# A fused attention and feed-forward kernel: the inverse roots of three norms in one chain of tensor-by-tensor steps, with new orders of work on all engines

## The reference

```python
x = x + _layernorm(_L0_attn_ref(_layernorm(x), Wq, Wk, Wv, Wp, bp, rel_table))
x = x + _layernorm(_L0_ffn_ref(_layernorm(x), W_r, W_k, W_v, mu_r, mu_k))
# attention, 16 heads of 64:
scores = einsum('bhtd,bhsd->bhts', q, k) * scale + bias[None]     # bias by clipped distance, causal
out = softmax(scores) @ v, then out @ Wp + bp
# feed-forward: x_prev is x one token earlier
r = sigmoid((mu_r * x + (1 - mu_r) * x_prev) @ W_r.T)
k = (mu_k * x + (1 - mu_k) * x_prev) @ W_k.T
out = r * (square(relu(k)) @ W_v.T)
# every norm:
(x - m) / sqrt(v + 1e-05)
```

## Time and profile before

| | us |
|---|---|
| median of 3 runs | 2222.81 |
| lowest and highest of them | 2222.11, 2223.51 |
| span of the profiled execution | 2224.4 |
| PE busy in it | 2111.2 (95%) |
| DVE busy | 1945.6 (87%) |
| POOL busy | 1697.1 (76%) |
| ACT busy | 1685.6 (76%) |

### The profile page before, as it was taken

The page is one execution under the profiler, slowest core; times in us unless marked ns, Lnnn a source line. Parts: engine busy times, 40 slices in busy tenths (PEclk is TensorE's granted clock), DMA queues, the critical chain, the costliest instruction groups (busy, mean ns, idle before and its releaser), DMA issues. The chain is left out here.

```text
span 2224.4 us, 75124 instructions
## 1 busy us (share of the span) xinstructions
PE 2111.2 (95%) x29456; PEld 1432.2 (64%) x29456; DVE 1945.6 (87%) x5210; ACT 1685.6 (76%) x2529; POOL 1697.1 (76%) x1372
## 2 busy tenths in 40 slices
PE   3798889999999999999999999999999999999986
PEld 1355556666676666667766666776666676666665
DVE  6777778999999999999999999999999998888857
ACT  2478788777878877887787788778877878877734
POOL 4376777788888888888888888888888887777752
PEclk9899999999999999999999999999999999999988
DMA  7111112232322323232232333223232322212251
GB/s 176 30 50 45 41 44 67 53 76 70 74 61 63 71 57 74 71 74 61 64 71 55 75 71 74 61 65 70 56 74 70 75 59 57 59 50 67 66 110 42
DMA packets 336784, 147.13 MB, mean 66 GB/s; under 512 B 172976, under 2 KB 335664, under 8 KB 336432
## 3 DMA queue, kind: packets, MB, share of 16 engines
q1 hardware_dynamic: 336432, 142.33, 26.9%
HBM read 24.25 MB, written 43.06 MB: 30 GB/s over the span
## 5 line engine op out<-in xcount | busy, mean ns | idle before, releaser
L1736 POOL TENSOR_TENSOR probs<-probs_f,probs 128x1024 f16<-128x1024 f32 (+3 forms) x704 | 1121.0, 1602 | 340.4 <-ACT probs L1002 338.0
L984 ACT ACTIVATE probs_f<-score_ps,score_unit 128x1024 f32<-128x1024 f32 (+3 forms) x704 | 620.6, 882 | 240.0 <-DVE score_ps L1293 114.9
L1277 DVE TENSOR_REDUCE row_max<-max_ps 128x2 f32<-128x1024 f32 (+2 forms) x640 | 632.4, 1005 | 17.2 <-PE max_ps L692 14.3
L1002 ACT CAST probs<-probs_f 128x1024 f16<-128x1024 f32 (+3 forms) x704 | 566.9, 814 | 12.3
L726 PEld LDWEIGHTS misc<-v_pair,probs 128*128 128x128 f16 x4608 | 415.0, 97 | 40.0 <-issue 29.1
L726 PE MATMUL misc<-v_pair,probs 128*128 128x65 f16 x4608 | 438.5, 194 | 0.6 <-issue 0.6
L727 PE MATMUL misc<-v_pair,probs 128*128 128x64 f16 x4608 | 436.8, 193 | 0.0
L728 PE MATMUL misc<-v_pair,probs 128*128 128x65 f16 x4608 | 435.9, 193 | 0.0
L728 PEld LDWEIGHTS misc<-v_pair,probs 128*128 128x128 f16 x4608 | 418.0, 97 | 0.0
L727 PEld LDWEIGHTS misc<-v_pair,probs 128*128 128x128 f16 x4608 | 417.9, 98 | 0.0
L616 PE MATMUL misc<-xT,w_split 128*128 128x512 f16 x1536 | 370.5, 385 | 7.2 <-DVE w_split L1396 3.8
(11 more groups left out here) (182 smaller groups left out, 3650.1 us busy)
## 6 DMA issues: line engine op xcount, KB each, us to landing
v_pair<-v_calc SPq DMA_DIRECT2D x64, 516.0 KB, 3.6
o_scratch<-o_stage SPq DMA_DIRECT2D x128, 256.0 KB, 2.5
xh<-x SPq DMA_DIRECT2D x56, 128.0 KB, 2.1
x_res<-x SPq DMA_DIRECT2D x56, 128.0 KB, 3.2
out<-out_sb SPq DMA_DIRECT2D x56, 128.0 KB, 1.7
shift_all<-shift_row SPq DMA_DIRECT2D x256, 1.0 KB
probs<-wqkv SPq DMA_DIRECT2D x1, 3072.0 KB, 13.2
probs<-band_scratch SPq DMA_DIRECT2D x8, 144.0 KB, 6.5
```

Source lines behind the costliest of these rows:

```text
L984: nc.scalar.activation(dst, score_ps[t % 2][:, :, 0:width], ACT.Exp, scale=score_unit[:]).then_inc(exp_done, 1)
L1002: nc.scalar.copy(dst, src).then_inc(hi_done, 1)
L1277: last = dve.tensor_reduce(dst[:, :, i % 4:i % 4 + 1], max_ps[:, :, col:col + width], AX.X, ALU.max)
L1736: pool.tensor_tensor(low, copy_of(par + ahead, t)[:, 0:2 * width], high, ALU.subtract).then_inc(lo_done_pool, 1)
```

## The change

1. **One chain for xh, x2 and z.** The mean and variance of the three now stand side by side in `mid_mv` (128 x 3 x 2), and one chain of 11 steps works on tiles of 128x3 (`mid_step`). Step 0 waits for all three statistics; where one of the three does not run yet, its column holds 1.0 from the start. POOL's `normalise` of all three waits for the end of this chain. The norm y keeps a chain of its own (`y_step`), also of 11 steps, on 128x1.
2. **Tensor by tensor.** A Newton round is three instructions: a = r*r and a = a*half (both `tensor_tensor`), r = (a + 1.5)*r (`scalar_tensor_tensor`). Step 0 is a `scalar_tensor_tensor` of the variance and a tile of -0.5*EPS. Only step 1, the guess, is still a `tensor_scalar` of one tensor. The empty instruction (`plain`) before each step is gone but for step 1.
3. **New orders.** The calls in the bodies of PE, ACT, DVE, POOL and SP stand in another order, and `TASKS` gives o2, o3, ffn, q0, q1, o0, o1, v0 other banks. The waits of the first steps move to the calls that need them.

```diff
-LN_OPS = 2 + 2 * NEWTON
+LN_OPS = 2 + 3 * NEWTON
+MIDDLE = ("xh", "x2", "z")
...
-TASKS = [("o2", 1, "prev"), ("o3", 0, "prev"), ("q0", 0, "qkv"), ("ffn", 1, "ffn"), ("o0", 1, "att"),
+TASKS = [("o2", 1, "prev"), ("ffn", 0, "ffn"), ("q0", 0, "qkv"), ("o3", 1, "prev"), ("q1", 1, "qkv"),
+         ("o0", 0, "att"), ("o1", 1, "att"), ("v0", 0, "qkv"), ("k0", 1, "qkv"), ("k1", 0, "qkv"),
...
-                dve.bn_aggr(mv[:], bn[:]).then_inc(aggr, 1)
-
-            def root_step(name, k, step):
-
-                _, mv, half_var, a, r = ln_bufs[name]
-                _, aggr, root, _ = ln_sems[name]
+                dve.bn_aggr(mv, bn[:]).then_inc(aggr, 1)
+
+            def root_step(root, k, step, var, half, a, r, eps):
+
+                if step > 0:
+                    dve.wait_ge(root, LN_OPS * k + step)
                 if step == 0:
-                    dve.wait_ge(aggr, k + 1)
+                    dve.scalar_tensor_tensor(half, var, -0.5, eps, ALU.mult, ALU.add).then_inc(root, 1)
+                elif step == 1:
+                    plain(dve)
+                    dve.tensor_scalar(r.bitcast(I32), half.bitcast(I32), -0.5, RSQRT_SEED, ALU.mult,
+                                      ALU.add).then_inc(root, 1)
+                elif step % 3 == 2:
+                    dve.tensor_tensor(a, r, r, ALU.mult).then_inc(root, 1)
+                elif step % 3 == 0:
+                    dve.tensor_tensor(a, a, half, ALU.mult).then_inc(root, 1)
                 else:
-                    dve.wait_ge(root, LN_OPS * k + step)
-                plain(dve)
-                if step == 0:
-                    dve.tensor_scalar(half_var[:], mv[:, 1:2], EPS, -0.5, ALU.add, ALU.mult).then_inc(root, 1)
-                elif step == 1:
-                    dve.tensor_scalar(r[:, 0:1].bitcast(I32), half_var[:].bitcast(I32), -0.5, RSQRT_SEED, ALU.mult,
-                                      ALU.add).then_inc(root, 1)
-                elif step % 2 == 0:
-                    at = step // 2 - 1
-                    dve.tensor_scalar(a[:], r[:, at:at + 1], r[:, at:at + 1], half_var[:], ALU.mult,
-                                      ALU.mult).then_inc(root, 1)
-                else:
-                    at = step // 2
-                    dve.tensor_scalar(r[:, at:at + 1], a[:], 1.5, r[:, at - 1:at], ALU.add, ALU.mult).then_inc(root, 1)
...
+                    dve.scalar_tensor_tensor(r, a, 1.5, r, ALU.add, ALU.mult).then_inc(root, 1)
+
+            def y_step(n, step):
+                g = n - PROJ_LAG
                 if step == 0:
...
+                    dve.wait_ge(ln_sems["y"][1], g + 1)
+                root_step(y_root, g, step, y_mv[:, 0, 1:2], y_half[:], y_a[:], y_r[:], mid_eps[:, 0:1])
+
+            def mid_step(n, step):
+                if step == 0:
+                    for name, part, lag in (("xh", "xt", -LEAD), ("x2", "mix", MIX_LAG), ("z", "ffn", FFN_LAG)):
+                        first, end = RANGES[part]
+                        if first <= n < end:
+                            dve.wait_ge(ln_sems[name][1], n - lag + 1)
+                        elif n == end:
+                            dve.wait_ge(ln_sems[name][3], n - lag)
+                root_step(mid_root, n + LEAD, step, mid_mv[:, :, 1:2].rearrange("p s o -> p (s o)"), mid_half[:],
+                          mid_a[:], mid_r[:], mid_eps[:])
...
+                    if n == -LEAD:
+                        find_wp_top()
```

More of the change, by code:

```diff
@@ L776, in body @@
                     ring = (m + LEAD // 2) // (NPAIR // 2) % 2 * T
+                    if has["next"]:
+                        fill(m, par, 0, at)
+                    if has["prev"]:
+                        weigh_values(2, m, par, 1, span)
+                    if has["ffn"]:
+                        tail_value(n, span)
                     if has["att"]:
@@ L779, in body @@
                     if has["next"]:
-                        ring = pe.snap(ring)
-                        if span.lo == -1:
-                            pe.wait_ge(ones_ready, 3)
-                            pe.wait_ge(band_scaled, 1)
-                        fill(m, par, 0, at)
+                        fill(m, par, 1, at)
+                    if has["qkv"]:
+                        project_qk("q0", n, pair * P, ring, span)
                     if has["prev"]:
-                        weigh_values(2, m, par, 1, span)
                         weigh_values(3, m, par, 1, span)
@@ L811, in body @@
                         transpose_maxima(0, n)
-                    if has["att"]:
-                        score(m, par, 0, 6, at)
+                    if has["qkv"]:
+                        project_qk("k0", n, pair * P, ring, span)
                     if has["next"]:
@@ L849, in body @@
                         transpose_maxima(1, n)
+                    if has["att"]:
+                        score(m, par, 0, 11, at)
+                    if has["next"]:
+                        score(m, par, 1, 0, at)
                 rolled(pe, span, body)
@@ L1036, in split_high, with split_wp_high @@
                                      scale=w_scale[:, i:i + 1]).then_inc(split_hi, 1)
+            def split_wp_high():
+                act.wait_ge(wp_setup, 6)
+                for k in range(2):
+                    nc.scalar.activation(wp_split[:, 0, 4 * k:4 * k + 4, :], wp_f32[k], ACT.Copy,
+                                         scale=wp_scale[:]).then_inc(wp_hi, 1)
             for i in SPLIT_ORDER:
@@ L1225, in roots @@
-            def roots(name, k):
-                for step in range(LN_OPS):
-                    root_step(name, k, step)
+                    dve.wait_ge(ln_sems["y"][1], g + 1)
[10 more added lines that the diff above has]
+                          mid_a[:], mid_r[:], mid_eps[:])
@@ L1469, in body @@
                     n = 2 * m + par
+                    if has["next"]:
+                        maxima(m, par, 1, 0)
+                    if n == WP_SPLIT + 1:
+                        scale_tail_weights()
                     if n == WP_SPLIT - 3:
@@ L1500, in body @@
                         low_part("q0", m, par, at)
+                        low_part("q1", m, par, at)
+                    if has["next"]:
+                        maxima(m, par, 1, 3)
+                    if has["att"]:
+                        outputs(0, m, par, 0)
+                        outputs(1, m, par, 0)
+                    if has["mix"]:
+                        statistics("x2", x2[(par + 1) % 2], n - MIX_LAG, x2_ready, n - MIX_LAG + 1)
+                    if has["ffn"]:
+                        statistics("z", z, n - FFN_LAG, z_ready, n - FFN_LAG + 1)
@@ L1541, in body @@
-                    if has["ffn"]:
-                        root_step("z", n - FFN_LAG, 2)
-                    if has["att"]:
-                        outputs(1, m, par, 0)
-                    if has["mix"]:
-                        root_step("x2", n - MIX_LAG, 5)
+                        low_part("k0", m, par, at)
+                    if has["xt"] or has["mix"] or has["ffn"]:
+                        mid_step(n, 4)
+                    if has["next"]:
+                        maxima(m, par, 1, 5)
@@ new lines, in body @@
+                    if has["xt"] or has["mix"] or has["ffn"]:
+                        mid_step(n, 5)
+                        mid_step(n, 6)
+                        mid_step(n, 7)
+                    if has["qkv"]:
+                        low_part("k1", m, par, at)
+                    if has["xt"] or has["mix"] or has["ffn"]:
+                        mid_step(n, 8)
+                        mid_step(n, 9)
+                        mid_step(n, 10)
+                    if has["next"]:
+                        maxima(m, par, 1, 6)
@@ L1547, in body @@
+                    if has["qkv"]:
+                        values_low("v1", m, par)
                     if has["att"]:
@@ L1680, in _ @@
             statistics("z", z, N - FFN_LAG, z_ready, N - FFN_LAG + 1)
-            roots("z", N - FFN_LAG)
             statistics("x2", x2[1], N - MIX_LAG, x2_ready, N - MIX_LAG + 1)
-            roots("x2", N - MIX_LAG)
+            for step in range(LN_OPS):
+                mid_step(N, step)
             last_projected(0)
@@ L1723, in _ @@
             last_gated(7)
-            roots("z", N + 1 - FFN_LAG)
+            for step in range(LN_OPS):
+                mid_step(N + 1, step)
             last_scales(2, 1, 5)
```

309 lines of the change are left out of this document (126 added, 183 removed).

## The result

The changed kernel takes **2546.8 us** (median of 4 runs, 2545.1 to 2548.0) against 2222.5 of before: a ratio of 1.146, 95% interval 1.1443 to 1.1476. The forecast was 2510, its range 2290 to 2690.

A forecast was written before the change was run, and what follows sets the result against it. PE was taken as the bound, DVE close behind. Full steps +259 us, early steps +31, last steps +4, start -5, end -2 sum to +287 on the 2224.4 us span, less 1.6: 2510 us, range 2290 to 2690.

The forecast's parts named there:

- The mechanism and the sign: DVE root steps reading two SBUF tensors wait for POOL's reading instructions, making the kernel slower (chance 0.84).
- The walk through the middle chain: DVE's new order laid over POOL's: middle-chain waits of 3.6 us per step, 3.45 of it reaching PE.
- fill f = 7 and the low half of v1: Where the middle chain's delay reaches PE: fill and output projection 3.45 us late per step.
- The y chain: At the step border, root steps wait 1.5 us for POOL's norm, low half and additions; 1.45 reaches PE.
- The two changes of mode fewer (-0.20): On PE, one block of 64-row groups fewer between full ones saves 0.20 us per step.
- the thin margins (+0.10): DVE's stretch up to maximum f = 6 and other tight places cost +0.1 us per step, between 0 and +0.3.
- 4.9 forecast: PE's lateness per full step: 3.45 us from the middle chain and 1.45 from the y chain.
- 4.8 forecast: Period of the 54 full steps rises 4.8 us, from 32.34 to 37.14, +259 us in all.
- n = 0 to 7: First eight steps: +0.5 us from new orders and 3.4 from middle-chain waits each, +31 us (0 to +50).
- For the start -5: DVE's first maximum no longer stands behind three `split_low` and two `wp_top` instructions: -5 us (-7 to 0).
- +4 - 2 = +2: From n = 62: y chain and last norms wait, +4 us; earlier output store and transposes at the end, -2.
- the 43 us: Extra y-chain waiting, 0.8 us in 54 steps, if POOL's norm held the lock throughout; would give 2553; not added.

The follow-up runs named there:

- experiments 3, 4 and 5: 3: before kernel with tensor-by-tensor root steps, 2486.6 us; 4: changed kernel, POOL writes zeros for low halves, 2322.9 us; 5: changed kernel, one-tensor steps without roots, 2226.8 us.
- free chains: Changed kernel with its new orders, but each root step reads one tensor of one column with immediate factors, inverse roots left out: 2226.8 us.
- experiment 10: Kernel before, with o1's weighing on PE behind fill f = 5, its DVE reading behind maximum f = 5, two Wp maxima moved: 2243.9 us.
- experiment 7: Changed kernel, with only the middle chain's guess over three columns split into three instructions of one column: 2538.5 us.

## Why the prediction was right, point by point

- **The mechanism and the sign.** Right. The waits for POOL's reads decide; experiments 3, 4 and 5 show it from three sides.
- **The walk through the middle chain.** It had 0.4 us at step 0, 1.2 at step 2 and 2.0 at step 3 or 4, 3.6 together. Measured: 0.44 at step 0, 1.36 at the guess (step 1), 1.9 at step 2, 3.7 together. The size was right, its place one step off: I took both guesses for free since they read one tensor. That holds for y's (145 ns) and not for the one over three columns.
- **The place on PE.** The walk let the loss arrive at fill f = 7 and the low half of v1. It arrives earlier, at the projection of v1, which takes the bank of k0: 135.2 of the 203.5 us of PE's idle time in the 54 steps. Row maxima end 51.4 us of the rest, and the bank of q0, which waits for the reading of z, 11.6. I had k0's low half in the list of DVE, and didn't look who waits for its bank.
- **The y chain.** 1.45 us per step were forecast for PE. On DVE it waits 63 us in 56 steps, 1.1 each; making it free gave 0.73 us per step. Mis-sized by a factor of two.
- **PE's own terms.** The two changes of mode fewer (-0.20) and the thin margins (+0.10) made 32.24 us for an unblocked step; free chains gave 32.28. Right in sum. The -0.20 by itself is not shown: PE's busy time per step is 32.20 us with free chains and 32.27 before, and experiment 10 lost it in waits.
- **What was missing: what a wait costs beyond its length.** PE idles 3.77 us per step, less than the 4.9 forecast. But it is also busy longer, 33.65 us per step against 32.27. Part is the last matmul ahead of a wait (mostly 0.32 to 0.38 us instead of 0.21 or less, 3.4 times a step, about 0.5 us by estimate). The rest fits the low clock after the long wait: the mean granted clock in the 54 steps is 0.97, with free chains 1.00. The two misses nearly cancel, and that is luck: the period averages 37.42 us, 5.0 above that of before, against 4.8 forecast.
- **n = 0 to 7.** +31 forecast, +50.6 measured. The waits gave 30.8 of it (against 27); the new orders gave 19.8 where I had 4. With free chains the granted clock there is 0.91, of before 0.98, and PE idles 33.5 us instead of 23.7. This term failed, and which of the new orders costs it no run shows.
- **Start and end.** For the start -5 was forecast, and from n = 62 on +4 - 2 = +2, of which the +4 are waits. Free chains gave -5.7 and -5.2, the changed kernel -1.0 and +0.6. There the gain of the start is gone by the same mechanism at its largest:

```profile
41.19 7.14 DVE L1224 SCALAR_TENSOR_TENSOR mid_half<-mid_mv,mid_eps 128x3 f32<-128x3 f32 x1
```

  beside POOL's preparation of the bias table:

```profile
40.95 8.03 POOL L1796 TENSOR_SCALAR bandT<-bandT,band_unit 128x2304 f32<-128x2304 f32 x1
```

- **When POOL's norm lets go.** The Trainium skill, "SBUF — State Buffer", section Who interferes with whom, has the lock held for the whole instruction. For POOL's TENSOR_TENSOR this case agrees: all 63 blocked r*r of the middle chain ended 0.01 to 0.02 us after it. For TENSOR_SCALAR it doesn't, as in the earlier trace rows: in the changed kernel all 48 two-tensor steps that a TENSOR_SCALAR of POOL held ended 0.65 or 0.66 us before it did (48.33 against 48.98 above). Not adding the 43 us was right. One reading in the prediction was off: at 2216.62 and 2216.82 POOL was not idle but in the last 0.62 us of its norm. The price of 0.16 us holds all the same.

## What to carry to other kernels

Count for each small VectorE instruction how many tensors it reads from SBUF, and on how many columns, before its own length: beside a GpSimd that reads much, a step of 0.16 us can cost 2 us, and a chain of dependent ones pays for each GpSimd instruction that it meets until the GpSimd itself has to wait. Fewer instructions in a form that waits for GpSimd are not cheaper than more in a form that doesn't. And taking one wait out of such a chain, or moving the other engine's work away, is to be checked against what meets it next: both were tried here, and gained next to nothing or lost 7%.

## What the runs showed of the hardware that I had not expected

- The guess on 128x3, a TENSOR_SCALAR with one tensor and immediate factors, waits for POOL (1261 ns on average, up to the end of the low half), the same on 128x1 never does (56 of y at 145 ns, none above 0.15 us; 204 of the middle chain in experiment 7 at 139 ns). The Trainium skill, "VectorE: DVE Perf Modes", section Mode 2×_2P — use both read ports for one tensor, says that such an instruction can stream its one tensor through both read ports; that would make it contend like a two-tensor one. The trace agrees in the waiting; no run here varied the number of columns between 1 and 3.
- Beside POOL's MEMSETs the two-tensor steps run freely (155 to 162 ns) and the guess on three columns waits, 64 times to 0.02 us after their end. Beside the TENSOR_SCALAR of 8.03 us shown above, the two-tensor step got through at 48.33 and the guess behind it only at 49.01, after the end at 48.98. So POOL's reading and its writing block different forms.
- After a wait of 2.5 us TensorE was granted 0.50 of its clock (1.2 GHz) from about 1039.5 to 1042.5, so that the matmuls behind the wait took twice their time. The clock had been at 1.00 during the idle time itself. PE's waits of 1.5 us at the border of this step were followed by 1.00.
